# Delta stage of a hybrid attention block: GpSimd's powers placed around the substitution, the diagonal blocks' rates one slot earlier

## The chip, the cores and the metric

The kernel runs on one core of one Trainium2 chip. The metric is the device time of one execution, in microseconds (us), the median of several runs. All data are float32. The engines are TensorE (PE in the profile), VectorE (DVE), ScalarE (ACT), GpSimd (POOL) and SyncE (SP), whose queue issues all the DMA transfers told of here. Each engine runs its own instructions strictly in the order in which they are written; engines meet only at semaphores.

## The reference, cut to what matters

The network is a chain of four residual blocks on (4, 1024, 128) data: a gated delta rule with its own feed-forward, two layers of local attention with feed-forward, a windowed attention, and the two layers once more. The change is in the first of them only, in its recurrent part:

```python
h = _rmsnorm(x, norm1_w)
q = _short_conv_silu(h @ Wq, conv_q_w).reshape(B, T, H, dk)      # H = 8, dk = 96, 4 taps
k = _short_conv_silu(h @ Wk, conv_k_w).reshape(B, T, H, dk)
v = _short_conv_silu(h @ Wv, conv_v_w).reshape(B, T, H, dv)      # dv = 192
q = _l2norm(q) * scale
k = _l2norm(k)
beta = sigmoid(h @ Wb)
g = -exp(A_log) * softplus(h @ Wa + dt_bias)

def step(S, inp):                                                # one token after the other
    q_t, k_t, v_t, g_t, b_t = inp
    S = S * exp(g_t)[..., None, None]
    v_old = einsum('bhk,bhkv->bhv', k_t, S)
    delta = (v_t - v_old) * b_t[..., None]
    S = S + einsum('bhk,bhv->bhkv', k_t, delta)
    return (S, einsum('bhk,bhkv->bhv', q_t, S))

o = _rmsnorm(o, onorm_w) * silu(h @ Wg)
x = x + o @ Wo
```

## The kernel before

**Tiling.** `delta_attention` (the function `delta_prepare` before it makes norms, rates and projections' weights) cuts the 4 x 1024 tokens into 32 chunks of 128 tokens; two chunks make a unit, so there are 16 units. Within a chunk the recurrence is solved as matrices: a triangular 128 x 128 system for each of 8 heads (its inverse ends in `tt`), then a short chain over the state `state`.

**Slots.** Every engine has one loop `for t in range(LAST)`. A unit has 28 slots (`SLOTS`), a chunk 14 (`HALF`); `unit(t, at)` gives the unit whose slot `at` is `t`, and `chunk(t, at)` the chunk, which starts 34 slots (`START`) behind its unit. A number above 27 or an `at` of a chunk therefore falls on some slot of a later unit: an `at` of 12 of a chunk falls on slots 4 and 18 of a unit, 14 on slots 6 and 20, 15 on 7 and 21, 16 and 17 on 8, 9, 22 and 23. In what follows "slot 20" is the slot `t` with remainder 20 by 28. In each slot one tile of k, q or v (8 + 8 + 12 tiles) is projected by TensorE (`L1299`), gets its four convolution taps, and is lit by ScalarE (`L1486`). ScalarE makes the product of the first tap (`L1466`) and of the last (`L1468`), VectorE adds the second and third (`L1623`, `L1631`), and GpSimd adds the last (`L1197`, semaphore `summed`). In slots 16 to 19 (`by_vector`) VectorE adds the last tap too (`L1628`), and GpSimd has no tile.

**What GpSimd does beside the tiles.** In those four slots it solves the 16 x 16 diagonal blocks of the unit's triangular systems (`solve_diagonal`, lines 1182 to 1190, 30 small instructions and a copy, written in four parts of which only the first waits for another engine, for `sub_rates`). Its result goes through memory: SyncE stores it (`L1137`) and loads it back into `t16`, `u16` and `tm`, and TensorE builds the inverse on it from slot 23 on. Further GpSimd raises three things to the power -1/2: the keys' norms `rn` (two halves of 8 columns, slots 15 and 16, `L1206`), and the output's norm `of` of each chunk (8 columns, slots 4 and 18, `L1226`). It makes `bm` for the inverse (slot 21, `L1213`, read by VectorE in slot 23), multiplies the output `o` by the gate in two halves (slots 6, 7, 20, 21; `L1221`, semaphore `o_gated`) and by `of` in two halves (slots 8, 9, 22, 23; `L1233`).

**Who waits for what.** In its slot `t` ScalarE runs `products_of(t)`, then `light(t-1)`, then its other work. Before it writes the gate of the next chunk (slots 8 and 22, `L1494`), it waits for both halves of `L1221`, since they read the gate before. Gate, `vt`, `kq` and the other side results share two banks of PSUM, `misc`, which go round by a table: TensorE claims a bank and waits until the engine that reads it has emptied it. So TensorE waits in slot 23 (`L1353`) for ScalarE's gate of slot 22. `project(t)` also waits for VectorE's taps of tile `t - 2`.

**The diagonal blocks' rates.** After slot 14 SyncE loads the diagonal blocks into `sub` (`L1127`), their diagonals into `n2k` in eight transfers (`L1131`), then `sub_beta` (`L1133`). VectorE turns `n2k` into rates for the whole chunk in slot 15 (`norms`, lines 1674 to 1681), and in slot 16 makes the rates of the diagonal blocks, `sub_rate`, with three small instructions at the end of its slot (`diagonal_rates`, lines 1697 to 1699), for which `solve_diagonal` waits.

Of the kernel before, what the change touches and what calls it, by code (L numbers as in the profile page):

```python
# [821 lines left out]
def delta_attention(nc, name, x_in, dst, w, c):  # L822
# [150 lines left out]
    def unit(t, at):  # L973

        n, rest = divmod(t - at, SLOTS)
        return n if rest == 0 and 0 <= n < UNITS else None
# [103 lines left out]
    def cols(cc):  # L1080
        return slice(cc * H, cc * H + H)

    with nc.Block() as block:

        @block.sync
        def _(sp):
# [15 lines left out]
            for t in range(LAST):  # L1102
# [20 lines left out]
                if n is not None:  # L1123
                    diag_out.need(sp, n)
                    sub_sb.need(sp, n - 1)
                    inv_out.need(sp, n - 1)
                    sp.dma_start(sub[:, 0], diag_d.rearrange("b c h j i -> (b c h) j i")).then_inc(diag_in.sem, 16)  # L1127
                    brk_sb.need(sp, n - 1)
                    for b in range(B16):
                        squares = diag_d[b].rearrange("c h j i -> (j i) (c h)")[0:256:17, :]  # L1130
                        sp.dma_start(n2k[16 * b:16 * b + 16, :], squares, allow_slow_non_contiguous=True).then_inc(n2k_in.sem, 16)  # L1131
                    betas = row_d[1, 2 * H * n:2 * H * (n + 1), :].rearrange("r (b i) -> b r i", i=16)
                    sp.dma_start(sub_beta[:], betas).then_inc(beta_in.sem, 16)  # L1133
# [25 lines left out]
        def _(pool):  # L1159
# [32 lines left out]
            for t in range(LAST):  # L1192
# [10 lines left out]
                for cc in range(2):  # L1203
                    n = unit(t, K_NORM + cc)
                    if n is not None:
                        ins = pool.tensor_tensor(rn[:, n % 2, cols(cc)], n2[:, n % 2, cols(cc)], minus_half[:, 0:H], ALU.pow)  # L1206
                        if cc == 1:
                            ins.then_inc(rn_sb.sem, 1)
                n = unit(t, K_NORM + 6)
                if n is not None:  # L1210
# [3 lines left out]
                                       merge[:].unsqueeze(1).to_broadcast([P, 2 * H, 32]), ALU.mult).then_inc(bm_sb.sem, 1)  # L1214
                for i in range(2):
# [6 lines left out]
                C = chunk(t, 12)  # L1222
                if C is not None:
                    ostat_step.need(pool, C)
                    o_normed.need(pool, C - 1)
                    pool.tensor_tensor(of[:], ostat[:, 1, :], minus_half[:, 0:H], ALU.pow).then_inc(of_sb.sem, 1)  # L1226
# [314 lines left out]
        def _(dve):  # L1541
# [149 lines left out]
            def diagonal_rates(t):  # L1691
                n = unit(t, SOLVE_AT)
# [1240 lines left out]
```

## Time and profile before

| what | us |
|---|---|
| median of 3 runs | 3790.98 |
| lowest and highest of them | 3790.16, 3799.99 |
| the profiled execution | 3798.17 |
| its span (first to last instruction) | 3795.2 |
| in it: before the units' loop | 92.0 |
| the delta stage's loop | 1548.0 |
| the other blocks | 2155.2 |
| TensorE busy over the span | 3294.0 (87%) |
| VectorE | 2723.1 (72%) |
| ScalarE | 2038.1 (54%) |
| GpSimd | 1804.8 (48%) |

Inside the loop (92 to 1640 us) TensorE is busy 1377.0 us, VectorE 1133.4, ScalarE 906.8 and GpSimd 790.2. The times of rows count from the start of the span. A row of the timeline gives the start, the duration, engine, line, operation, what is written and read, shape and count, and in brackets how long the engine sat idle before it and what released it. The shares over the whole kernel say little here: the four engines take turns in being late, slot by slot, so the stretch around one unit's substitution has to be read instruction by instruction.

### The profile page before, as it was taken

To read this page: it belongs to the slowest core of one execution; us is meant where nothing else is said; L and a number is where in the kernel's file an instruction comes from. 1 tells how busy PE (TensorE), PEld (TensorE's weight loads), DVE (VectorE), ACT (ScalarE), POOL (GpSimd) and SP (SyncE) were. 2 spreads that over 40 slices of the span, in tenths; PEclk is the share of its full clock that TensorE was granted. 3 is DMA by queue.
4 is the path that set the end of the run, shared out by engine and by line. 5 is a ranking of instruction groups with operands and counts; after the bars stand their busy time and mean duration, and the time that the engine had idled before them with its cause. 6 is when DMAs were issued, how large, how long until landed. Compare 5 with 4: busy or idle time off the path is not lost. (4 is left out here: it accounts for less than half of the span.)

```text
span 3795.2 us, 87218 instructions
## 1 busy us (share of the span) xinstructions
PE 3294.0 (87%) x32714; PEld 2466.9 (65%) x32714; DVE 2723.1 (72%) x5753; ACT 2038.1 (54%) x4599; POOL 1804.8 (48%) x1647
## 2 busy tenths in 40 slices
PE   4789999999999999968999999986898599899998
PEld 3577777777777777745666566654666366656665
DVE  5577777777777777647777677775999477767775
ACT  3456565656565656513666366632444366636662
POOL 3355555555555555434666166632122466526662
PEclk8689999999999999989999999997999799999999
DMA  4111111111111111033122321222112222131122
GB/s 123 23 24 25 25 25 25 26 25 26 24 27 24 27 25 24 11 95 81 43 53 56 93 50 44 71 79 55 47 50 55 63 49 64 45 95 44 46 71 70
DMA packets 409630, 182.71 MB, mean 48 GB/s; under 512 B 235808, under 2 KB 384384, under 8 KB 406656
## 3 DMA queue, kind: packets, MB, share of 16 engines
q1 hardware_dynamic: 409216, 177.15, 19.0%
q8 instruction: 265, 4.34, 0.5%
q14 instruction: 149, 1.22, 0.1%
HBM read 94.47 MB, written 40.12 MB: 35 GB/s over the span
## 5 line engine op out<-in xcount | busy, mean ns | idle before, releaser
L1197 POOL TENSOR_TENSOR delta_cv<-delta_cv,delta_last_tap 96x256 f32<-96x256 f32 (+1 forms) x384 | 332.7, 867 | 623.4 <-DVE delta_cv L1631 623.4
L1938 POOL TENSOR_TENSOR g_a_rn<-g_a_clip,g_minus_half 128x16 f32<-128x16 f32 x64 | 186.4, 2912 | 271.2 <-DVE g_a_clip L2202 243.0
L1938 POOL TENSOR_TENSOR f_a_rn<-f_a_clip,f_minus_half 128x16 f32<-128x16 f32 x64 | 186.3, 2911 | 260.7 <-DVE f_a_clip L2202 232.5
L2155 ACT ACTIVATE g_a_pr<-g_ps,g_a_nb,g_a_rn 128x128 f32<-128x128 f32 x512 | 185.5, 468 | 146.4 <-DVE g_a_nb L2236 146.4
L2155 ACT ACTIVATE f_a_pr<-f_ps,f_a_nb,f_a_rn 128x128 f32<-128x128 f32 x512 | 185.5, 468 | 146.4 <-DVE f_a_nb L2236 146.4
L1466 ACT ACTIVATE delta_cv<-delta_ps,delta_conv_qk 96x256 f32<-96x256 f32 x256 | 120.9, 472 | 253.5 <-PE delta_ps L1299 252.7
L1623 DVE SCALAR_TENSOR_TENSOR delta_cv<-delta_ps,delta_conv_qk,delta_cv 96x256 f32<-96x256 f32 x256 | 122.1, 477 | 169.5 <-ACT delta_last_tap L1468 169.2
L1243 PE MATMUL delta_ps<-delta_state,delta_qk 96*128 96x192 f32 x1024 | 199.4, 339 | 27.3 <-issue 22.8
L1623 DVE SCALAR_TENSOR_TENSOR delta_cv<-delta_ps,delta_conv_v,delta_cv 128x256 f32<-128x256 f32 x192 | 92.1, 480 | 155.5 <-ACT delta_last_tap L1468 154.1
L1243 PEld LDWEIGHTS delta_ps<-delta_state,delta_qk 96*128 96x128 f32 x1024 | 168.3, 193 | 41.7 <-issue 38.1
L1466 ACT ACTIVATE delta_cv<-delta_ps,delta_conv_v 128x256 f32<-128x256 f32 x192 | 90.5, 471 | 127.5 <-PE delta_ps L1299 127.5
L1486 ACT ACTIVATE delta_vt<-delta_cv 128x256 f32<-128x256 f32 x192 | 80.0, 417 | 136.5 <-DVE delta_cv L1631 84.7
L1941 POOL TENSOR_TENSOR f_a_rot_c<-f_a_rot_c,f_a_rot_s 128x1024 f32<-128x1024 f32 x64 | 150.8, 2357 | 0.0
L1941 POOL TENSOR_TENSOR g_a_rot_c<-g_a_rot_c,g_a_rot_s 128x1024 f32<-128x1024 f32 x64 | 150.8, 2356 | 0.0
L1299 PE MATMUL delta_ps<-delta_ht,delta_wv 128*128 128x259 f32 x384 | 127.7, 423 | 23.6 <-DVE delta_cv L1631 23.6
L2190 DVE TENSOR_TENSOR g_a_rot_c<-g_ps,g_a_table 128x512 f32<-128x512 f32 x128 | 87.8, 686 | 76.5 <-PE g_ps L1972 72.7
L2190 DVE TENSOR_TENSOR f_a_rot_c<-f_ps,f_a_table 128x512 f32<-128x512 f32 x128 | 87.8, 686 | 74.4 <-PE f_ps L1972 70.2
L2230 DVE TENSOR_REDUCE g_a_nmx<-g_ps 128x8 f32<-128x1024 f32 x64 | 78.4, 1225 | 87.5 <-PE g_ps L2028 87.5
L1972 PE MATMUL g_ps<-g_a_wqkv,g_a_ht 128*128 128x512 f32 x256 | 129.9, 631 | 10.8 <-DMA g_a_scales<-L_ffn_k_scale 9.5
L2230 DVE TENSOR_REDUCE f_a_nmx<-f_ps 128x8 f32<-128x1024 f32 x64 | 78.4, 1225 | 84.0 <-PE f_ps L2028 84.0
L1308 PE MATMUL delta_ps<-delta_wg,delta_ht 128*128 128x512 f32 x192 | 100.0, 617 | 38.3 <-ACT delta_vr L1512 38.3
L1631 DVE SCALAR_TENSOR_TENSOR delta_cv<-delta_ps,delta_conv_qk,delta_cv 96x256 f32<-96x256 f32 x256 | 122.9, 480 | 9.1
(350 smaller groups left out, 10477.3 us busy)
## 6 DMA issues: line engine op xcount, KB each, us to landing
f_a_vm<-f_a_v SPq DMA_DIRECT2D x128, 130.0 KB, 2.3
g_a_vm<-g_a_v SPq DMA_DIRECT2D x128, 130.0 KB, 2.3
delta_gd<-delta_dram_row SPq DMA_DIRECT2D x16, 1024.0 KB, 4.6
window_vm<-window_v SPq DMA_DIRECT2D x64, 128.0 KB, 2.3
f_m_x<-y SPq DMA_DIRECT2D x24, 256.0 KB, 3.5
delta_dram_inv<-delta_sub SPq DMA_DIRECT2D x16, 256.0 KB, 2.1
f_m_more<-x SPq DMA_DIRECT2D x16, 256.0 KB, 3.9
x<-f_m_x SPq DMA_DIRECT2D x16, 256.0 KB, 2.3
```

The source lines that it names most:

```text
L1197: pool.tensor_tensor(cv[0:M, t % 3], cv[0:M, t % 3], last_tap[0:M, t % 3], ALU.add).then_inc(summed.sem, 1)
L1243: mm = pe.matmul(ps[0:M, 2 * i + j // 2, j % 2 * DV:(j % 2 + 1) * DV], lhs(h), rhs(h), start=True, stop=True)
L1299: mm = pe.matmul(ps[0:rows_of(k), conv_bank(t), 0:3 + U], lhs, ht[:, n % 3], start=True, stop=True)
L1466: e = act.activation(cv[0:M, t % 3], ps[0:M, conv_bank(t), 0:U], ACT.Copy, scale=taps[:, 0:1])
L1623: dve.scalar_tensor_tensor(out=mine, in0=ps[0:M, conv_bank(t), 1:1 + U], scalar=wts[:, 1:2], in1=mine, op0=ALU.mult, op1=ALU.add).then_inc ...
L1631: dve.scalar_tensor_tensor(out=mine, in0=ps[0:M, conv_bank(t), 2:2 + U], scalar=wts[:, 2:3], in1=mine, op0=ALU.mult, op1=ALU.add).then_inc ...
L1938: pool.tensor_tensor(rn[:, u % 2], clip[:, u % 2], minus_half[:], ALU.pow).then_inc(rn_sb.sem, 1)
L1941: pool.tensor_tensor(rot[:, u % 2], rot_c[:, u % 2], rot_s[:, u % 2], ALU.add).then_inc(rot_sb.sem, 1)
L1972: mm = pe.matmul(ps[:, QK + n, :], tokens, wqkv[:, n * INNER:(n + 1) * INNER], start=True, stop=True)
L2155: e = act.activation(pr[:, u % 2, half, i, :], ps[:, score_bank(u, half), i * P:(i + 1) * P], ACT.Exp, bias=nb[:, u % 2, half, i:i + 1], s ...
L2190: dve.tensor_tensor(rot_c[:, u % 2, r * H:(r + 1) * H, :], ps[:, QK + r, :].rearrange("p (h i) -> p h i", i=DH), cos, ALU.mult)
L2230: dve.tensor_reduce(nmx[:, u % 2].rearrange("p e i -> p (e i)"), ps[:, b0:b0 + 2, :].rearrange("p e (i k) -> p (e i) k", k=P), AX.X, ALU.m ...
```

## The change

Five pieces, all in `delta_attention`; later lines move up by five. `rn` becomes one power over both halves (16 columns) in slot 15. `of` moves from slot 18 and 4 to slot 20 and 6, where it stands ahead of the product with the gate. `bm` moves from slot 21 to slot 22. VectorE makes the diagonal blocks' rates in slot 15, behind `norms`. SyncE loads `sub_beta` ahead of the eight transfers of `n2k`.

```diff
@@ sync
                     sp.dma_start(sub[:, 0], diag_d...).then_inc(diag_in.sem, 16)
+                    betas = row_d[1, 2 * H * n:2 * H * (n + 1), :].rearrange("r (b i) -> b r i", i=16)
+                    sp.dma_start(sub_beta[:], betas).then_inc(beta_in.sem, 16)
                     brk_sb.need(sp, n - 1)
                     for b in range(B16):
                         squares = ...
                         sp.dma_start(n2k[16 * b:16 * b + 16, :], squares, ...).then_inc(n2k_in.sem, 16)
-                    betas = ...
-                    sp.dma_start(sub_beta[:], betas).then_inc(beta_in.sem, 16)
@@ gpsimd
                     n2k_sb.need(pool, n)
                     bvr_sb.need(pool, n - 2)
-                for cc in range(2):
-                    n = unit(t, K_NORM + cc)
-                    if n is not None:
-                        ins = pool.tensor_tensor(rn[:, n % 2, cols(cc)], n2[:, n % 2, cols(cc)], minus_half[:, 0:H], ALU.pow)
-                        if cc == 1:
-                            ins.then_inc(rn_sb.sem, 1)
-                n = unit(t, K_NORM + 6)
+                    pool.tensor_tensor(rn[:, n % 2], n2[:, n % 2], minus_half[:], ALU.pow).then_inc(rn_sb.sem, 1)
+                n = unit(t, K_NORM + 7)
                 if n is not None:
                     rates_sb.need(pool, n)
                     copied(pool, ("x4", n - 1, 1))
                     pool.tensor_tensor(bm[:], ...).then_inc(bm_sb.sem, 1)
+                C = chunk(t, 14)
+                if C is not None:
+                    ostat_step.need(pool, C)
+                    o_normed.need(pool, C - 1)
+                    pool.tensor_tensor(of[:], ostat[:, 1, :], minus_half[:, 0:H], ALU.pow).then_inc(of_sb.sem, 1)
                 for i in range(2):
                     C = chunk(t, 14 + i)
                     ...
-                C = chunk(t, 12)
-                if C is not None:
-                    ostat_step.need(pool, C)
-                    o_normed.need(pool, C - 1)
-                    pool.tensor_tensor(of[:], ...).then_inc(of_sb.sem, 1)
@@ vector
             def diagonal_rates(t):
-                n = unit(t, SOLVE_AT)
+                n = unit(t, SOLVE_AT - 1)
```

GpSimd, unit 1, from the end of the substitution (the copy) to slot 23. `delta_cv` is the addition of a tile's last tap, `delta_o<-delta_o,delta_gate` the product with the gate, `delta_o<-delta_o,delta_of` that with the norm. Before, with the power `delta_of` of this stretch standing 8 rows further up, inside the substitution:

```order
L1190 COPY delta_sub<-delta_sub 128x256
L1197 TENSOR_TENSOR delta_cv<-delta_cv,delta_last_tap 128x256
L1221 TENSOR_TENSOR delta_o<-delta_o,delta_gate 128x768
L1197 TENSOR_TENSOR delta_cv<-delta_cv,delta_last_tap 128x256
L1213 TENSOR_TENSOR delta_bm<-delta_nbrk,delta_merge 128x512
L1221 TENSOR_TENSOR delta_o<-delta_o,delta_gate 128x768
L1197 TENSOR_TENSOR delta_cv<-delta_cv,delta_last_tap 128x256
L1233 TENSOR_TENSOR delta_o<-delta_o,delta_of 128x768
```

and now:

```order
L1190 COPY delta_sub<-delta_sub 128x256
L1197 TENSOR_TENSOR delta_cv<-delta_cv,delta_last_tap 128x256
L1214 TENSOR_TENSOR delta_of<-delta_ostat,delta_minus_half 128x8
L1221 TENSOR_TENSOR delta_o<-delta_o,delta_gate 128x768
L1197 TENSOR_TENSOR delta_cv<-delta_cv,delta_last_tap 128x256
L1221 TENSOR_TENSOR delta_o<-delta_o,delta_gate 128x768
L1197 TENSOR_TENSOR delta_cv<-delta_cv,delta_last_tap 128x256
L1208 TENSOR_TENSOR delta_bm<-delta_nbrk,delta_merge 128x512
L1228 TENSOR_TENSOR delta_o<-delta_o,delta_of 128x768
```

Between the copy and the second product with the gate `delta_bm` has left and the power `delta_of` has come.

VectorE, unit 2, slots 15 and 16. `delta_n`, `delta_brk`, `delta_nbrk` belong to `norms`, `delta_state` is the update of the state, the three rows on `delta_cv` are one tile's taps. Before:

```order
L1677 TENSOR_TENSOR delta_brk<-delta_inv,delta_ex 128x16
L1680 TENSOR_SCALAR delta_nbrk<-delta_brk 128x16
L1681 SCALAR_TENSOR_TENSOR delta_npb<-delta_brk,delta_ex 128x16
L1583 SCALAR_TENSOR_TENSOR delta_state<-delta_state,delta_ex,delta_ps 96x192 x4
L1623 SCALAR_TENSOR_TENSOR delta_cv<-delta_ps,delta_conv_v,delta_cv 128x256
L1628 SCALAR_TENSOR_TENSOR delta_cv<-delta_ps,delta_conv_v,delta_cv 128x256
L1631 SCALAR_TENSOR_TENSOR delta_cv<-delta_ps,delta_conv_v,delta_cv 128x256
L1697 TENSOR_SCALAR delta_sub_rate<-delta_sub 128x16
L1698 RECIPROCAL delta_sub_rate<-delta_sub_rate 128x16
L1699 SCALAR_TENSOR_TENSOR delta_sub_rate<-delta_sub_rate,delta_sub_beta 128x16
```

and now:

```order
L1675 TENSOR_SCALAR delta_nbrk<-delta_brk 128x16
L1676 SCALAR_TENSOR_TENSOR delta_npb<-delta_brk,delta_ex 128x16
L1692 TENSOR_SCALAR delta_sub_rate<-delta_sub 128x16
L1693 RECIPROCAL delta_sub_rate<-delta_sub_rate 128x16
L1694 SCALAR_TENSOR_TENSOR delta_sub_rate<-delta_sub_rate,delta_sub_beta 128x16
L1578 SCALAR_TENSOR_TENSOR delta_state<-delta_state,delta_ex,delta_ps 96x192 x4
L1618 SCALAR_TENSOR_TENSOR delta_cv<-delta_ps,delta_conv_v,delta_cv 128x256
L1623 SCALAR_TENSOR_TENSOR delta_cv<-delta_ps,delta_conv_v,delta_cv 128x256
L1626 SCALAR_TENSOR_TENSOR delta_cv<-delta_ps,delta_conv_v,delta_cv 128x256
```

The three instructions of the rates have moved ahead of one half of the state's update (four instructions) and of one tile's taps.

## Rows read from the trace of the kernel before

**Rows 1.** Stretches of two neighbouring units: length, busy us, granted clock (PEclk), DMA share, GB/s.

```profile
842.30:933.90 91.60, 82.74 (x774) 70.72 (x773) 70.74 (x150) 57.01 (x144) 49.87 (x68) 0.98 0.12 26
933.90:1030.00 96.10, 87.04 (x774) 74.43 (x773) 72.08 (x156) 57.00 (x144) 49.90 (x68) 0.93 0.12 25
```

**Rows 2.** Timeline of GpSimd, unit 7, slots 15 and 16.

```profile
769.57 1.65 POOL L1206 TENSOR_TENSOR delta_rn<-delta_n,delta_minus_half 128x8 f32<-128x8 f32 x1
773.31 0.73 POOL L1182 TENSOR_TENSOR delta_sub<-delta_sub,delta_sub_rate 128x256 f32<-128x256 f32 x1 [2.10 <-DVE delta_sub_rate L1699]
...
776.00 1.65 POOL L1206 TENSOR_TENSOR delta_rn<-delta_n,delta_minus_half 128x8 f32<-128x8 f32 x1
```

**Rows 3.** Timeline of GpSimd, unit 7, slot 18 to slot 21.

```profile
783.51 1.65 POOL L1226 TENSOR_TENSOR delta_of<-delta_ostat,delta_minus_half 128x8 f32<-128x8 f32 x1
...
787.23 0.61 POOL L1190 COPY delta_sub<-delta_sub 128x256 f32<-128x256 f32 x1
787.80 0.73 POOL L1197 TENSOR_TENSOR delta_cv<-delta_cv,delta_last_tap 128x256 f32<-128x256 f32 x1
788.48 1.81 POOL L1221 TENSOR_TENSOR delta_o<-delta_o,delta_gate 128x768 f32<-128x768 f32 x1
790.25 0.72 POOL L1197 TENSOR_TENSOR delta_cv<-delta_cv,delta_last_tap 128x256 f32<-128x256 f32 x1
790.93 1.05 POOL L1213 TENSOR_TENSOR delta_bm<-delta_nbrk,delta_merge 128x512 f32<-128x512 f32 x1
791.93 1.81 POOL L1221 TENSOR_TENSOR delta_o<-delta_o,delta_gate 128x768 f32<-128x768 f32 x1
```

**Rows 4.** Timeline of ScalarE there, slots 21 and 22.

```profile
788.56 0.42 ACT L1486 ACTIVATE delta_vt<-delta_cv 128x256 f32<-128x256 f32 x1 [2.36 <-POOL delta_cv L1197]
...
793.78 1.08 ACT L1494 ACTIVATE delta_gate<-delta_ps 128x512 f32<-128x512 f32 x2 [2.35 <-POOL delta_o L1221]
```

**Rows 5.** The waits, 280 to 1580 us: total us, times, longest.

```profile
ACT delta_gate L1494 <- POOL delta_o L1221: 43.6, 28, 2.4
```

**Rows 6.** Timeline of TensorE there, slot 23.

```profile
794.52 0.52 PE L1353 MATMUL delta_ps<-delta_ident,delta_vt 128*128 128x128 f32 x3 [0.66 <-ACT delta_gate L1494]
```

**Rows 7.** Timeline of VectorE, unit 7, slots 15 and 16.

```profile
768.73 0.16 DVE L1674 TENSOR_SCALAR delta_n<-delta_n2k 128x16 f32<-128x16 f32 x1
...
769.67 0.17 DVE L1680 TENSOR_SCALAR delta_nbrk<-delta_brk 128x16 f32<-128x16 f32 x1
...
772.57 0.16 DVE L1697 TENSOR_SCALAR delta_sub_rate<-delta_sub 128x16 f32<-128x16 f32 x1
```

**Rows 8.** The same, the last adding instruction of tiles 20 and 21.

```profile
784.66 0.48 DVE L1631 SCALAR_TENSOR_TENSOR delta_cv<-delta_ps,delta_conv_v,delta_cv 128x256 f32<-128x256 f32 x1
...
787.33 0.48 DVE L1631 SCALAR_TENSOR_TENSOR delta_cv<-delta_ps,delta_conv_v,delta_cv 128x256 f32<-128x256 f32 x1
```

**Rows 9.** The DMA issues of SyncE, unit 7, slot 15.

```profile
761.62 3.87 SPq L1131 DMA_DIRECT2D delta_n2k<-delta_dram_diag  x8
765.53 0.60 SPq L1133 DMA_DIRECT2D delta_sub_beta<-delta_dram_row  x1
```

**Rows 10.** The page, costliest groups: a power over 16 columns in another stage.

```profile
L1938 POOL TENSOR_TENSOR f_a_rn<-f_a_clip,f_minus_half 128x16 f32<-128x16 f32 x64 | 186.3, 2911 | 260.7 <-DVE f_a_clip L2202 232.5
```

**Rows 11.** Stretches of 4 us with the granted clock, units 7 and 8.

```profile
790.00:794.00 4.00, 3.86 (x12) 2.71 (x10) 0.97 (x2) 0.97 (x3) 4.00 (x5) 0.62 0.27 26
...
822.00:826.00 4.00, 4.00 (x46) 3.22 (x43) 3.96 (x9) 3.39 (x10) 2.25 (x2) 0.50 0.00 0
```

**Rows 12.** Timeline of all engines, unit 9, slots 7 to 9.

```profile
933.97 0.72 POOL L1197 TENSOR_TENSOR delta_cv<-delta_cv,delta_last_tap 96x256 f32<-96x256 f32 x1 [1.40 <-DVE delta_cv L1631]
...
936.51 1.09 ACT L1494 ACTIVATE delta_gate<-delta_ps 128x512 f32<-128x512 f32 x2 [0.77 <-POOL delta_o L1221]
...
940.68 1.74 DVE L1600 TENSOR_SCALAR delta_q_eps<-delta_q_sum 128x8 f32<-128x8 f32 x1
...
940.93 1.46 POOL L1233 TENSOR_TENSOR delta_o<-delta_o,delta_of 128x768 f32<-128x768 f32 x1
```

More of the change, by code:

```diff
@@ L1131, in _ @@
                         sp.dma_start(n2k[16 * b:16 * b + 16, :], squares, allow_slow_non_contiguous=True).then_inc(n2k_in.sem, 16)
-                    betas = row_d[1, 2 * H * n:2 * H * (n + 1), :].rearrange("r (b i) -> b r i", i=16)
-                    sp.dma_start(sub_beta[:], betas).then_inc(beta_in.sem, 16)
                 n = unit(t, SOLVE_AT + 4)
@@ L1221, in _ @@
                         pool.tensor_tensor(mine, mine, gate[:, HB * i * DV:HB * (i + 1) * DV], ALU.mult).then_inc(o_gated.sem, 1)
-                C = chunk(t, 12)
-                if C is not None:
-                    ostat_step.need(pool, C)
-                    o_normed.need(pool, C - 1)
-                    pool.tensor_tensor(of[:], ostat[:, 1, :], minus_half[:, 0:H], ALU.pow).then_inc(of_sb.sem, 1)
                 for i in range(2):
```

## The prediction

> **What bounds the kernel now.** The page's shares name no single engine, so I read the delta stage's loop in units. Two neighbouring units take 91.6 and 96.1 us with the same work [rows 1]; that difference is taken up under the clock. Then I read one unit (unit 7) engine by engine from slot 15 to slot 23, looking for the engine that never waits. It is GpSimd. It starts the substitution at 773.31 after 2.10 us of idleness, in which it waits for VectorE's rates [rows 2], and from there it has no idle time until its second product with the gate ends at 791.93 + 1.81 = 793.74 [rows 3]. Two others wait for it: ScalarE stands 2.36 us for tile 20's last tap and 2.35 us for that second product before it may write the gate, at 793.78 [rows 4], and TensorE's next work of slot 23 starts at 794.52, released by ScalarE's gate [rows 6]. The wait of the gate occurs 28 times in 1300 us, twice a unit, 43.6 us in all [rows 5]: 2.35 us here, and 0.77 us in slot 8 [rows 12]. So around the substitution the time of a slot is set by the length of GpSimd's list, and the last wait is that of ScalarE's gate in slot 22.
>
> **Part 1, the substitution itself.** It runs from 773.31 to 787.23 + 0.61 = 787.84, 14.53 us [rows 2, 3]. Two powers of 1.65 us lie in it, the second half of `rn` at 776.00 and `of` at 783.51. Without them 14.53 - 3.30 = 11.23 us remain. The new start: one power over 16 columns takes the place of 8 columns at 769.57. The kernel has that shape elsewhere with 2.91 us [rows 10]; the bounds are 1.65 us (a column count that costs nothing) and 3.30 us (twice the 8 columns). I take 2.91, the row of the same shape: 769.57 + 2.91 = 772.48. The rates are no longer waited for: `norms` is past its fourth instruction at 769.67 and two more follow [rows 7], so the rates, 0.74 us long by the distance from 772.57 to GpSimd's start at 773.31, are there at about 770.7. End of the substitution: 772.48 + 11.23 = 783.71, 4.1 us earlier; by the bounds 782.4 to 784.1.
>
> **Part 2, what is late next.** Not all of the 4.1 us count. GpSimd's next instruction adds tile 20's last tap, for which VectorE must end at 784.66 + 0.48 = 785.14 [rows 8]. VectorE works without a break over slots 16 to 19, and the rates only change places in its list, so I leave that time. GpSimd now idles about 1.4 us there; this also covers either bound of the 16-column power. Then come, back to back: tap 20 (0.73), `of` (1.65), first product (1.81), tap 21 (0.72; its input ends at 787.81, long before), second product (1.81) [rows 3, 8]. That is 6.72 us, ending at 785.14 + 6.72 = 791.86. Before, it was 793.74. `bm` (1.05 us) has left this list for slot 22. **Gain: 1.88 us a unit.** Had `of` been left out of this list too, it would be 3.5; the change gives 1.65 us of it back. The stretch after slot 22 is a shifted copy: ScalarE's gate starts 1.88 us earlier, TensorE's slot 23 as well. `bm` would end near 791.86 + 0.73 + 1.05 = 793.6, and VectorE reads it in slot 23, after TensorE's work that follows 794.52 - 1.88 = 792.64 and ScalarE's tile in between, so I cost its move at nothing; the cover is about 1 us. Units 1 to 15 have chunk work in slots 20 and 21 (unit 0 has none and is counted at zero): 15 x 1.88 = **28.2 us**.
>
> **Part 3, the small moves.** VectorE's rates in slot 15 push one half of the state's update and tile 16's taps back by 0.74 us, and nothing after them, since the rates stood there anyway. Who waits: TensorE's transposes of slot 17. Bound 0 to 0.74 us a unit; I take 0, because VectorE runs without idle time through slot 19 and is what the others wait for there. SyncE issues `sub_beta` 0.60 us long ahead of eight transfers that now end at 765.49 and then at 766.09 [rows 9]; VectorE reads them at 768.73 [rows 7] without a wait. Cost 0, at most 0.6. In slots 4 to 9 the power `of` leaves slot 4 and stands ahead of the product in slot 6: GpSimd's 1.40 us of idleness ahead of tile 7 [rows 12] take up most of 1.65 us, 0.25 us are left to reach the gate of slot 8, which already waits 0.77 us for GpSimd. Bounds 0 and 1.65 us a unit; I take 0, since 0.25 us is less than the slack of the tiles around it (TensorE's projection is the next wait of ScalarE). Both ends stay in the range.
>
> Does a small VectorE instruction stand still beside a GpSimd power? The trace has both answers. `L1680` starts at 769.67, inside the power that began at 769.57, and takes 0.17 us [rows 7, 2]; `L1600` starts at 940.68 and takes 1.74 us, until GpSimd's 768-column product of 940.93 is over at 942.39 [rows 12]. The rates have the form of `L1680`, and their neighbour is a power, so I take 0.17. The Trainium skill (SBUF — State Buffer, Who interferes with whom) says that VectorE's `tensor_scalar` in a two-port mode shares a port pair with GpSimd, which is held for the whole instruction. By that rule the time would be that of rival D; the row of `L1600` agrees with it for long products, the row of `L1680` does not for powers.
>
> **Part 4, the clock.** Granted clock drops twice in a unit's neighbourhood. One low stretch falls on slots 21 to 22 (mean 0.62 of full in 790 to 794, 2.4 GHz being full and 1.2 GHz the low level), after TensorE stood still; it costs nothing now, since TensorE waits for the gate anyway. A second one (0.50 in 822 to 826) [rows 11] comes after the tiny matrices of the inverse in slots 2 and 3, and only in every other unit: it is the difference between 96.1 and 91.6 us, 4.5 us [rows 1]; seven of the units 1 to 14 have it. The work is the same in both, so where it falls depends on how the units lie in time, and a unit 1.9 us shorter moves it. Bounds: in no unit (-7 x 4.5 = -31.5 us) and in all 15 (+8 x 4.5 = +36 us). I take 4 of 15, -13.5 us: the present order looks like a lock that brings it back each second unit, and without that lock it should be rarer. Against this, TensorE's idle time in slots 22 to 23 is now over sooner and the first low stretch can reach work on the path; 4 us at 0.62 lose 4 x 0.38 = 1.5 us [rows 11]. Bounds 0 to 1.5 us a unit, I take a third, 0.55: +8.3 us. The clock together: -5 us.
>
> **The sum.** 28.2 + 5.2 = 33.4 us off. The profiled execution took 3798.17 us, 7.2 over the median of the runs; this gives 3764.8 for it and 3790.98 - 33.4 = **3757.6 us** for the median.
>
> **Rivals.** (A) The second low stretch goes altogether and the first stays harmless: 28.2 + 31.5 = 59.7 us off, 3731. For it speaks that one half of the units are free of it already at the same work; against it that the low activity in slots 2 and 3 stays. Chance 0.17. (B) GpSimd's gain is given back at another place. In slot 23 GpSimd would run product, tap and product back to back (1.46 + 0.73 + 1.46 us), and `L1600`, which falls there, could stand for two of them; or `of` in slot 6 reaches the gate of slot 8 with more than 0.25 us. With 1.4 us a unit returned, 15 x 0.48 = 7 us stay: 3784. Against it speaks that VectorE has idle time behind `L1600`. Chance 0.18. (C) Slower: the low clock falls on slots 2 to 5 in every unit and on TensorE's path in slot 23 as well, +36 + 15 x 1.5 = +58.5 us against 28.2: 3821. It decides in this direction from 28 us of clock loss on; for it, that the pattern of today is kept by the units' length, which changes; against it, that both must come together. Chance 0.06. (D) The rates stand still beside the power as `L1600` does beside a product. Then they begin at 772.48 instead of 769.9, VectorE's whole list of slots 16 to 20 is 2.5 us late, tile 20's taps with it, and 1.88 - 2.5 = -0.6 us a unit are left: 15 x 0.6 = 9 us more, less 5 for the clock, 3795. The row of `L1680` speaks against it, the unbroken list of VectorE for its price. Chance 0.08.
>
> **How the numbers follow.** The forecast, 3745 to 3772, has 0.51. The range takes it in, rival A down to its price and rival B up to a little over its price: 3731 to 3786. A measurement of this kernel can tell 0.3%, 11.4 us, from no change. Faster by more than that (under 3779.6): the forecast, A and half of B, 0.77. Within it: half of B and D, 0.17. Slower: C, 0.06.
>
> **What would show it.** Right: GpSimd's substitution starts without a wait for the rates and is over about 4 us sooner against the taps of tile 20; a new idle time of 1 to 1.5 us ahead of tile 20's last tap; ScalarE's wait for tile 20 gone, its wait for the gate in slot 22 still there and about 1.9 us earlier; units without the second low stretch near 89.7 us. Wrong: a 16-column power well over 3.3 us, `L1692` (the rates' first instruction) far longer than 0.17 us, a wait of `bm`'s reader in slot 23, or units that differ in length in another pattern than by 4.5 us.

## The result, and the profile after

The kernel after takes 3778.45 us (median of 8 runs, 3757.21 to 3786.40), the kernel before beside it 3796.11 us (8 runs, 3786.49 to 3802.89). The ratio is 0.9948 with an interval of 0.9927 to 0.9969: faster by 0.5%, 17.7 us by the medians. The forecast was 33.4 us off, 3757.6 us. The direction is right and the time lies in the range of 3731 to 3786, but not in its middle part, 3745 to 3772; about half of the gain is missing. The profiled execution of after took 3786.40 us with a span of 3784.6 us. It is the slowest of the eight, 8 us above their median.

**The units.** The same view as in [rows 1], stretches with their busy times and granted clock, for units of after. A unit runs here from the end of one substitution's copy to the end of the next.

```profile
961.10:1054.90 93.80, 85.08 (x779) 72.93 (x778) 71.64 (x155) 57.48 (x146) 49.52 (x68) 0.96 0.12 26
1147.70:1237.50 89.80, 81.08 (x775) 69.39 (x774) 71.92 (x155) 57.08 (x146) 49.52 (x68) 1.00 0.13 26
1237.50:1333.30 95.80, 88.42 (x773) 76.23 (x772) 71.07 (x149) 56.97 (x145) 49.48 (x67) 0.91 0.12 25
```

The unit from 1147.70 has full clock throughout and takes 89.8 us, where 89.7 was forecast and 91.6 stood in [rows 1]. But of the units 1 to 14 only three are within 1 us of that; the others take 91.5 to 97.6 us, where before there were 91.6 and 96.1 and one of 97.8. The steps of the change are read in the undisturbed unit first.

**The power and the rates, slot 15.** Timeline of GpSimd, after; then of VectorE at the same place.

```profile
1132.85 0.72 POOL L1197 TENSOR_TENSOR delta_cv<-delta_cv,delta_last_tap 96x256 f32<-96x256 f32 x1 [2.34 <-DVE delta_cv L1626]
1133.53 2.91 POOL L1203 TENSOR_TENSOR delta_rn<-delta_n,delta_minus_half 128x16 f32<-128x16 f32 x1
1136.41 0.72 POOL L1182 TENSOR_TENSOR delta_sub<-delta_sub,delta_sub_rate 128x256 f32<-128x256 f32 x1
```

```profile
1133.17 0.43 DVE L1672 TENSOR_TENSOR delta_brk<-delta_inv,delta_ex 128x16 f32<-128x16 f32 x1
1133.63 0.17 DVE L1675 TENSOR_SCALAR delta_nbrk<-delta_brk 128x16 f32<-128x16 f32 x1
...
1133.81 0.17 DVE L1692 TENSOR_SCALAR delta_sub_rate<-delta_sub 128x16 f32<-128x16 f32 x1
...
1134.29 0.17 DVE L1694 SCALAR_TENSOR_TENSOR delta_sub_rate<-delta_sub_rate,delta_sub_beta 128x16 f32<-128x16 f32 x1
```

The 16-column power takes the 2.91 us of [rows 10]; the substitution (`L1182`) starts right behind it, with no bracket for an idle time, where it had waited 2.10 us [rows 2]. The three rates run inside the power at 0.17 and 0.25 us.

**Slots 20 to 22.** GpSimd, after, from the substitution's copy on: to be held against [rows 3].

```profile
1147.10 0.61 POOL L1190 COPY delta_sub<-delta_sub 128x256 f32<-128x256 f32 x1
1149.20 0.73 POOL L1197 TENSOR_TENSOR delta_cv<-delta_cv,delta_last_tap 128x256 f32<-128x256 f32 x1 [1.49 <-DVE delta_cv L1626]
1149.88 1.66 POOL L1214 TENSOR_TENSOR delta_of<-delta_ostat,delta_minus_half 128x8 f32<-128x8 f32 x1
1151.50 1.83 POOL L1221 TENSOR_TENSOR delta_o<-delta_o,delta_gate 128x768 f32<-128x768 f32 x1
1153.27 0.75 POOL L1197 TENSOR_TENSOR delta_cv<-delta_cv,delta_last_tap 128x256 f32<-128x256 f32 x1
1153.96 1.83 POOL L1221 TENSOR_TENSOR delta_o<-delta_o,delta_gate 128x768 f32<-128x768 f32 x1
1155.72 0.74 POOL L1197 TENSOR_TENSOR delta_cv<-delta_cv,delta_last_tap 128x256 f32<-128x256 f32 x1
1156.40 1.07 POOL L1208 TENSOR_TENSOR delta_bm<-delta_nbrk,delta_merge 128x512 f32<-128x512 f32 x1
```

GpSimd, which never waited here, now stands 1.49 us for VectorE ahead of tile 20. From there to the end of the second product, 1149.20 to 1155.79, the list is 6.59 us long. ScalarE beside it, to be held against [rows 4]:

```profile
1150.06 0.41 ACT L1481 ACTIVATE delta_vt<-delta_cv 128x256 f32<-128x256 f32 x1
...
1154.05 0.42 ACT L1481 ACTIVATE delta_vt<-delta_cv 128x256 f32<-128x256 f32 x1 [2.22 <-POOL delta_cv L1197]
1155.82 1.09 ACT L1489 ACTIVATE delta_gate<-delta_ps 128x512 f32<-128x512 f32 x2 [1.35 <-POOL delta_o L1221]
```

The wait for tile 20 is gone (the first row), a wait of 2.22 us for tile 21 has come, because `of` and a product stand ahead of its last tap, and the gate's own wait is 1.35 instead of 2.35 us. Rows of the waits over 280 to 1580 us, the first of before, the other two of after. The last answers to [rows 5]; the wait of TensorE for the gate has grown from 7.1 to 34.6 us:

```profile
PE delta_ps L1353 <- ACT delta_gate L1494: 7.1, 14, 0.7
...
PE delta_ps L1348 <- ACT delta_gate L1489: 34.6, 14, 2.6
ACT delta_gate L1489 <- POOL delta_o L1221: 31.1, 27, 1.4
```

**TensorE around slot 23.** This is where the missing half is. First before, unit 7, TensorE ahead of and behind the row of [rows 6]:

```profile
789.65 1.12 PE L1308 MATMUL delta_ps<-delta_wg,delta_ht 128*128 128x512 f32 x2 [2.70 <-ACT delta_vr L1512]
790.61 2.39 PE L1243 MATMUL delta_ps<-delta_vr,delta_tt 128*128 128x192 f32 x8
792.79 1.07 PE L1299 MATMUL delta_ps<-delta_ht,delta_wv 128*128 128x259 f32 x2
...
795.01 1.12 PE L1365 MATMUL delta_ps<-delta_t,delta_al 64*64 64x32 f32 x32
796.06 1.57 PE L1243 MATMUL delta_ps<-delta_vr,delta_tt 128*128 128x192 f32 x8
```

Then after, the undisturbed unit:

```profile
1151.15 1.13 PE L1303 MATMUL delta_ps<-delta_wg,delta_ht 128*128 128x512 f32 x2 [0.23 <-ACT delta_vr L1507]
...
1156.56 0.52 PE L1348 MATMUL delta_ps<-delta_ident,delta_vt 128*128 128x128 f32 x3 [2.55 <-ACT delta_gate L1489]
1157.05 1.12 PE L1360 MATMUL delta_ps<-delta_t,delta_al 64*64 64x32 f32 x32
1158.10 1.57 PE L1238 MATMUL delta_ps<-delta_vr,delta_tt 128*128 128x192 f32 x8
1159.51 0.60 PE L1294 MATMUL delta_ps<-delta_ht,delta_wv 128*128 128x259 f32 x2
```

And the same rows of after in the unit of 93.8 us, with its stretches of 4 us and their granted clock:

```profile
970.82 0.52 PE L1348 MATMUL delta_ps<-delta_ident,delta_vt 128*128 128x128 f32 x3 [2.55 <-ACT delta_gate L1489]
971.31 1.85 PE L1360 MATMUL delta_ps<-delta_t,delta_al 64*64 64x32 f32 x32
973.09 2.93 PE L1238 MATMUL delta_ps<-delta_vr,delta_tt 128*128 128x192 f32 x8
```

```profile
968.00:972.00 4.00, 1.45 (x20) 1.03 (x20) 0.78 (x3) 2.34 (x6) 4.00 (x5) 0.93 0.36 37
972.00:976.00 4.00, 4.00 (x31) 3.94 (x29) 1.49 (x4) 1.52 (x4) 3.26 (x3) 0.50 0.13 33
```

Before, TensorE stood 2.70 us ahead of slot 21's work and only 0.66 us ahead of slot 23 [rows 6]. The low clock of [rows 11] followed the long wait and fell on products (2.39 us where 1.57 is the full-clock time) that were over before the gate came. After, the first wait has shrunk to 0.23 us, and the long one, 2.55 us, stands directly ahead of slot 23. TensorE is busy 1.45 of the 4 us from 968, and then the clock is 0.50, which is the 1.2 GHz level, on work that all other engines wait for: the inverse's 32 small matmuls take 1.85 instead of 1.12 us, the eight products 2.93 instead of 1.57.

**A third stretch.** The record of the granted clock has one more low stretch, 80 to 93 us behind the end of the substitution, around the next substitution (slots 16 to 19). Before, none of the units 1 to 14 has it; after, nine have. It makes TensorE's projections late, ScalarE's products of the last tap with them, and so VectorE's taps of tile 20. VectorE in after ahead of tile 20, first in front of the unit from 961.1, with this stretch, then in front of the undisturbed one:

```profile
962.39 0.48 DVE L1618 SCALAR_TENSOR_TENSOR delta_cv<-delta_ps,delta_conv_v,delta_cv 128x256 f32<-128x256 f32 x1 [1.38 <-ACT delta_last_tap L1463]
...
1148.11 0.48 DVE L1618 SCALAR_TENSOR_TENSOR delta_cv<-delta_ps,delta_conv_v,delta_cv 128x256 f32<-128x256 f32 x1 [0.90 <-ACT delta_last_tap L1463]
```

GpSimd's wait for tile 20 is then 1.9 to 3.2 us instead of 1.5, in seven of the 14 units, 5.8 us in all; it is 2.34 us in the unit of 93.8 us.

### The profile page after: what moved, and what is told of

Read it like the earlier page. It is cut to its first block and busy times, and to the rows that moved or that the text cites. A ratio compares the mean times of both kernels' runs of the same rounds, so it can differ in the third digit from the quotient of the medians.

```text
span 3784.6 us, 87201 instructions
## 1 busy us (share of the span) xinstructions
PE 3303.1 (87%) x32714; PEld 2481.1 (66%) x32714; DVE 2725.0 (72%) x5753; ACT 2038.9 (54%) x4599; POOL 1798.9 (48%) x1631
## 5 line engine op out<-in xcount | busy, mean ns | idle before, releaser
L1967 PE MATMUL f_ps<-f_a_wqkv,f_a_ht 128*128 128x512 f32 x256 | 129.0, 627 | 0.0
```

The source lines that it names most:

```text
L1967: mm = pe.matmul(ps[:, QK + n, :], tokens, wqkv[:, n * INNER:(n + 1) * INNER], start=True, stop=True)
```

## Experiments

In each table row below the ratio is against the kernel before, measured beside it; times of different rows are compared by these ratios.

| label | what it is | median us | ratio (interval) |
|---|---|---|---|
| after_again | the kernel after | 3771.93 | 0.9960 (0.9942 to 0.9978) |
| f_before | before + fillers | 3795.53 | 1.0001 (0.9989 to 1.0013) |
| f_after | after + fillers | 3764.83 | 0.9921 (0.9908 to 0.9935) |
| f_ofback | f_after, `of` at its old place | 3744.28 | 0.9864 (0.9851 to 0.9877) |
| f_bmback | f_after, `bm` in slot 21 again | 3774.08 | 0.9947 (0.9934 to 0.9961) |
| f_rates | rates and load of `sub_beta` moved alone, + fillers | 3757.98 | 0.9898 (0.9885 to 0.9912) |
| f_powers | powers, `bm` and that load moved, rates not, + fillers | 3762.42 | 0.9910 (0.9896 to 0.9923) |
| p_rates | rates and load moved alone | 3762.09 | 0.9929 (0.9916 to 0.9941) |
| ofback | after, `of` at its old place | 3725.57 | 0.9815 (0.9800 to 0.9829) |
| g_ofback | ofback + one filler | 3725.99 | 0.9808 (0.9790 to 0.9826) |
| g_after | after + one filler | 3769.86 | 0.9953 (0.9939 to 0.9967) |
| g2_after | after + two fillers | 3755.20 | 0.9889 (0.9872 to 0.9905) |

### Fillers in both kernels: f_before, f_after

Two theories on the missing half: the clock took it, or GpSimd's gain is returned at another place (rival B). To tell them apart both kernels get fillers: products that nobody reads, written to columns of PSUM that are written anew before anyone reads them. They stand where TensorE stood still or did little, ahead of tile 23 and ahead of the products of slots 2 and 5. For `y5`, one of these products, the claim of the bank is also moved ahead of two waits.

```diff
@@ tensor, ahead of the projection of tile t; k is the tile's number
+                if k == 23:
+                    for r in range(2):
+                        pe.matmul(ps[:, conv_bank(t), :], ident[:], wg[:, r * 512:(r + 1) * 512], start=True, stop=True)
@@ tensor, product y, behind its claim of a bank; the same in y5
+                    pe.matmul(ps[:, bank, 256:512], ident[:], wg[:, 0:256], start=True, stop=True)
```

> The kernel before, with extra TensorE products whose results nobody reads, put where TensorE waits in any case: two of 512 columns ahead of tile 23, one of 256 columns ahead of the last product y, one of 256 ahead of each y5. They are to hold the granted clock at its full level through the loop. Theory (GpSimd's list, and beside it the clock): without the low stretches of slots 2 to 5 every unit takes what the clean units took, 91.6 us, plus some tenths for the fillers; 7 x 4.5 us less and more at the start, about 3765 (1.008 times faster). Rival (the length of units isn't the clock's doing): fillers only add, 3796 to 3810.

> The changed kernel with the same fillers. Theory (GpSimd's list is 1.88 us shorter in each of 15 units, and in the plain kernels the clock takes half of it back): 28 us under the filled kernel before, units of 89.7 to 90 us throughout, about 3735. Rival 1 (the gain is only another pattern of the clock): the same time as the filled kernel before, within 5 us. Rival 2 (the list gives only what the plain kernels differ by, 1.2 us a unit): 18 us less.

f_before takes 3795.53 us: no gain over before, where about 3765 was looked for. The fillers do remove the stretch of slots 2 to 5 from all of units 1 to 14, but they cost 1.3 us in every unit (92.9 against 91.6 us, all of it in slots 2 to 5), and in five units the low stretch of slots 21 and 22 is still there and runs into the fillers, which makes them 94.1 us. Together this eats the gain. As a remedy it is a miss. As an instrument it works in the main: the stretch of slots 2 to 5 and that on slot 23 are gone from the units 1 to 14 of both kernels, though the clock is not the same everywhere, since f_after has the third stretch in seven units. Units of f_before, f_after, f_ofback, f_bmback, f_rates and f_powers:

```profile
596.88:689.77 92.89, 84.88 (x784) 71.40 (x784) 71.94 (x157) 57.21 (x144) 49.86 (x70) 1.00 0.12 26
```

```profile
766.87:857.87 91.00, 86.00 (x786) 72.97 (x785) 71.95 (x155) 57.13 (x146) 49.41 (x68) 0.98 0.13 26
```

```profile
853.86:943.81 89.95, 84.56 (x786) 71.45 (x785) 70.71 (x150) 57.22 (x144) 49.55 (x69) 1.00 0.12 27
```

```profile
682.76:774.74 91.98, 84.81 (x786) 71.37 (x785) 71.86 (x155) 56.99 (x146) 49.46 (x68) 1.00 0.12 26
```

```profile
491.87:582.67 90.80, 84.81 (x785) 71.40 (x785) 70.70 (x150) 57.23 (x145) 49.81 (x70) 1.00 0.12 26
```

```profile
584.68:675.78 91.10, 84.88 (x786) 71.41 (x785) 72.05 (x156) 57.11 (x145) 49.45 (x68) 1.00 0.12 26
```

f_after against f_before: 1.9 us a unit, between these two as between the means of all 14 (93.3 and 91.4), and 30.7 us by the medians. The 1.88 us of the prediction's Part 2 and its 28.2 us are there in full when the low clock is kept off slots 2 to 5 and 23. Nothing of them is returned elsewhere: rival B falls, and the missing half is the clock's.

### One piece undone: f_ofback, f_bmback

```diff
@@ gpsimd, f_ofback: the power stands behind the product with the gate, in slot 18
-                C = chunk(t, 14)
+                C = chunk(t, 12)
@@ gpsimd, f_bmback
-                n = unit(t, K_NORM + 7)
+                n = unit(t, K_NORM + 6)
```

> The filled changed kernel with the power `of` back in slots 4 and 18 (behind its old neighbours), all else as changed. Theory: in slot 18 it is covered by GpSimd's 1.4 us of idleness ahead of tile 20, in slot 20 it isn't. The substitution ends 1.65 us later, tile 20 starts 0.2 later, and the second product with the gate ends 1.4 us earlier than in the changed kernel: up to 1.4 x 15 = 21 us under the filled changed kernel, less if VectorE's taps of tile 22 or ScalarE are then late (they allow at least 1 us). Rival (moving `of` out of the substitution is what makes the gain): slower by 1.65 x 15 = 25 us.

> The filled changed kernel with `bm` back in slot 21, ahead of the second product with the gate. Theory: 1.05 us more in the list for which ScalarE waits, 15 x 1.05 = 16 us over the filled changed kernel. Rival (the wait of ScalarE's gate is no longer on the path after the change): no difference within 4 us.

With `of` back in slot 18, inside the substitution, a unit is 1.0 us shorter than in f_after, and the time is 20.5 us less (3744.28 against 3764.83 us). The substitution is 12.9 instead of 11.3 us long, but that only fills the 1.5 us in which GpSimd waited for tile 20, and `of` is gone from the list behind it. In the profiled executions the units carry 12.9 us of this; another 7.8 us come behind the last substitution, which was not followed up. So moving `of` harms. The merging of `rn` was not undone by itself. With `bm` back in slot 21, ahead of the second product, the gate waits for it again. ScalarE, f_bmback:

```profile
783.88 1.09 ACT L1494 ACTIVATE delta_gate<-delta_ps 128x512 f32<-128x512 f32 x2 [2.35 <-POOL delta_o L1221]
```

That is 1.0 us a unit, the length of `bm`, as costed. By the medians it is only 9.3 us, not some 16; the profiled spans differ by 14.7 us (3779.4 and 3764.7), so the units carry it, and the medians' difference is smaller than they explain.

### Each half of the change alone: f_rates, f_powers

```diff
@@ f_rates: before + beta's load first, and in the vector part
-                n = unit(t, SOLVE_AT)
+                n = unit(t, SOLVE_AT - 1)
@@ f_powers: after, but the rates in slot 16 as before
-                n = unit(t, SOLVE_AT - 1)
+                n = unit(t, SOLVE_AT)
```

> The filled kernel before (fillers as in the other filled kernels) with one part of the change: the diagonal blocks' rates in slot 15 and the load of sub_beta first. Powers and bm as before. Theory (GpSimd's list): the substitution starts at the end of the first half of rn, 2.1 us earlier, and everything behind it in the list moves with it, since tile 20's taps are not reached: 2.1 us a unit under the filled kernel before, units of 90.8 us against 92.9 and 91.0 of the filled change, about 3795 - 31 = 3764: this part alone gives all that the change gives. Rival (the parts add up, each its own share): 0.83 us a unit, the share by which the start of the substitution moved in the changed kernel, units of 92.1 us, about 3782.

> The filled changed kernel with the rates back in slot 16: only the powers and bm moved (and sub_beta loaded first). Theory: the substitution starts at 773.3 as before on the scale of unit 7 and ends at 784.6, still ahead of the taps of tile 20 at 785.1; the list behind is the same: 91.0 us a unit, the time of the filled changed kernel within 3 us. Rival (the parts add up): 0.8 us a unit slower than the filled changed kernel, 12 us more.

Either half gives what both give: units of 90.8 and 91.1 us, against 91.0 for the whole (f_after) and 92.9 for f_before. Two rows say why the halves don't add. GpSimd at tile 20 in f_rates, then in f_powers:

```profile
582.63 0.73 POOL L1197 TENSOR_TENSOR delta_cv<-delta_cv,delta_last_tap 128x256 f32<-128x256 f32 x1
```

```profile
676.54 0.72 POOL L1197 TENSOR_TENSOR delta_cv<-delta_cv,delta_last_tap 128x256 f32<-128x256 f32 x1 [0.75 <-DVE delta_cv L1631]
```

f_rates takes away only the 2.10 us wait of [rows 2], keeps the substitution at 14.5 us, and reaches tile 20 without idle time. f_powers still waits 0.8 to 1.2 us for the rates and nevertheless stands 0.75 us ahead of tile 20; the whole change stands 1.5 us there. VectorE's last adding instruction of tile 20 is the floor of f_powers and of the whole change. f_rates comes 0.5 us behind it (it is over at 582.13) and has no `of` behind it in its list.

### Without fillers: ofback, p_rates, after_again

> The changed kernel once more, to stand beside the next two on the same chip: 3770 to 3785, clean units of 89.75 us, most units 2 to 6 us longer, with a low clock in slots 23 and 24.

> No fillers: the changed kernel with the power `of` back in slots 4 and 18. Theory: its clean units are 1.0 us shorter than those of the changed kernel (88.7), as in the filled pair (90.0 against 91.0), so 15 to 20 us under 3778 if the clock takes the same part, about 3760; where the low stretches fall can move that by 20 us either way. Rival (the clock eats every gain of this kind): 3778.

> Without fillers: the kernel before with the rates in slot 15 and sub_beta loaded first, nothing else. Theory: clean units of 91.6 - 2.1 = 89.5 us, so never worse in GpSimd's list than the full change (89.75); with the clock as it falls, 3750 to 3785. Rival (only the full change brings a gain on this kernel): within 5 us of the kernel before.

ofback, which is the kernel after with `of` back at its old place and nothing else, is with g_ofback the fastest of all: 3725.57 us, 0.9815 (0.9800 to 0.9829) of before, and the version to keep. A unit of it, and TensorE in slot 23:

```profile
1112.47:1200.79 88.32, 81.02 (x775) 69.33 (x773) 71.41 (x156) 57.04 (x144) 49.52 (x69) 1.00 0.13 27
```

```profile
1118.33 0.52 PE L1348 MATMUL delta_ps<-delta_ident,delta_vt 128*128 128x128 f32 x3 [1.13 <-ACT delta_gate L1489]
```

Its undisturbed unit is 1.4 us shorter than that of after, and TensorE's wait ahead of slot 23 is 1.4 us shorter too, 1.13 us. Fifteen units at 1.4 us are 21 us. By the ratios ofback is 1.3 to 1.5% ahead of after, 50 to 55 us. The rest, some 30 us, is in the main clock that ofback doesn't lose: by the table further down, 16.7 us are lost in it, where after loses 53.5 and 37.6. p_rates, measured beside after_again, is ahead of it too, 3762.09 to 3771.93 us (0.9929, 0.9916 to 0.9941, and 0.9960, 0.9942 to 0.9978), although its undisturbed unit (89.5 us) is much the same as that of after; its wait in slot 23 is 2.0 us.

### The wait itself: g_after, g2_after, g_ofback

If TensorE's wait of 2.55 us ahead of slot 23 brings the low clock onto that slot, then filling it with work that nobody reads, and changing nothing else, must give the time back. g_after and g_ofback have one filler of 512 columns ahead of tile 23, g2_after two.

```diff
@@ tensor, ahead of the projection of tile t: g_after, g_ofback; g2_after has the line for wg[:, 512:1024] too
+                if k == 23:
+                    pe.matmul(ps[:, conv_bank(t), :], ident[:], wg[:, 0:512], start=True, stop=True)
```

> The changed kernel with `of` back and one filler only, a product of 512 columns ahead of tile 23, where TensorE waits. Theory (the clock is lost at two places, after slot 22 and after slots 2 and 3, and the fillers in slots 2, 3 and 5 cost 1.3 us a unit): the low stretch after slot 22 goes at no cost, that after slots 2 and 3 stays in some units; 3740 to 3755. Rival (only the fillers of slots 2, 3 and 5 hold the clock): 3760 as without fillers.

> The changed kernel with one filler: a product of 512 columns ahead of tile 23, in the 2.5 us in which TensorE waits for the gate. Theory (the gain that is missing was lost because TensorE's wait in slots 22 and 23 is followed by a low clock, now on the path): the low stretch at +10 us from the end of the substitution goes in most units, those units shorten by 2 to 4 us, and 20 to 35 us come off the changed kernel, about 3750. Rival (the missing gain was lost somewhere else, in slots 6 to 9 or at the moved bm): the filler changes nothing beyond 5 us, since it only fills a wait.

> The changed kernel with both 512-column products ahead of tile 23 and none of the other fillers. With one of them the low stretch at +10 us stayed in 8 of 14 units; with both and the others it was in none. Theory (the low clock at +10 us is the answer to TensorE's wait in slots 22 and 23): it is gone from at least 12 of 14 units, and clean units stay at 89.8 to 90.3 us; the stretch at +37 us comes in some units with 4.5 us each, so 3745 to 3762. Rival (the fillers of slots 2, 3 and 5 held the clock, not those ahead of tile 23): the stretch at +10 us stays in half of the units, 3765 to 3775.

One filler missed: g_after takes 3769.86 us, no different from after_again (3771.93), where 3750 was expected. Two fillers hit: 3755.20 us, 0.9889 (0.9872 to 0.9905) of before, against 0.9960 for after_again. TensorE in g2_after, slot 22 to slot 23:

```profile
857.31 1.88 PE L1292 MATMUL delta_ps<-delta_wg,delta_ident 128*128 128x512 f32 x4
859.02 0.60 PE L1297 MATMUL delta_ps<-delta_ht,delta_wv 128*128 128x259 f32 x2
860.44 0.52 PE L1351 MATMUL delta_ps<-delta_ident,delta_vt 128*128 128x128 f32 x3 [0.81 <-ACT delta_gate L1492]
860.93 1.12 PE L1363 MATMUL delta_ps<-delta_t,delta_al 64*64 64x32 f32 x32
861.98 1.57 PE L1238 MATMUL delta_ps<-delta_vr,delta_tt 128*128 128x192 f32 x8
```

The gate comes as late as before the fillers; only the time until then is filled, and slot 23 runs at full clock. In g_ofback the filler changes nothing (3725.99), since there the wait was short already; it is 0.3 us with it.

Over all kernels without fillers in slots 2 and 5 the wait and the low clock on slot 23 go together. The wait alone does not decide it, though: f_bmback, with all fillers, still waits 1.8 us ahead of slot 23 and has the low clock there in none of 14 units, where g_after with 1.7 us has it in 8. The last three columns count units 1 to 14 of the profiled executions by the record of the granted clock: low about 8 to 12 us behind the substitution's end (slots 22 to 24), low about 33 to 39 us behind it (slots 2 to 5), and the time lost, which is the length of the 14 units less 14 undisturbed ones and has the third stretch in it. The wait is the usual one; some units of before and of ofback have half of it. The undisturbed unit of before, 91.6 us, has the low stretch of slots 21 and 22, which costs it nothing.

| kernel | wait ahead of slot 23, us | low at slot 23 | low at slots 2 to 5 | lost, us |
|---|---|---|---|---|
| after | 2.55 | 11 | 5 | 53.5 |
| after_again | 2.55 | 11 | 2 | 37.6 |
| p_rates | 2.0 | 8 | 2 | 26.9 |
| g_after | 1.7 | 8 | 3 | 31.9 |
| ofback | 1.1 | 1 | 2 | 16.7 |
| g2_after | 0.8 | 0 | 2 | 14.1 |
| g_ofback | 0.3 | 0 | 3 | 18.7 |
| before | 0.7 | 1 | 7 | 33.4 |

(1310.7 - 14 x 89.8 = 53.5 for after; 1315.8 - 14 x 91.6 = 33.4 for before.) In g_after and p_rates the low stretches on slot 23 are all of the shorter kind, over in about 3 us; in after five of the eleven are twice as long.

## Why the prediction was half right

**Part 1, right.** The power over 16 columns took 2.91 us as taken from [rows 10], and the substitution 11.3 us (11.23 forecast). It starts without a wait.

**Part 2, right, and to the tenth.** Idle time ahead of tile 20: 1.49 us (about 1.4 forecast). The list behind it: 6.59 us (6.72). The undisturbed unit: 89.8 us (89.7). With fillers in both kernels, 1.9 us a unit and 30.7 us in all (1.88 and 28.2). The remark that leaving `of` out of the list would give 3.5 us a unit was right as well: it gives 3.3 us (91.6 to 88.3, ofback) and 2.9 us under fillers (92.9 to 89.95, f_ofback). What the prediction did not see is that with `of` moved the halves of the change overlap, so that either alone carries nearly all of it.

**Part 3, right.** In slot 8 ScalarE waits 0.94 us for the product with the gate, 0.17 more than in [rows 12]; 0.25 was the estimate and 1.65 the upper bound.

```profile
1202.68 1.08 ACT L1489 ACTIVATE delta_gate<-delta_ps 128x512 f32<-128x512 f32 x2 [0.94 <-POOL delta_o L1221]
```

`bm` is over at 1157.47, and VectorE reads it at 1158.58 (`L1703`), so its cover was 1.1 us (about 1). The rates cost 0.17 us beside the power; over all 16 units `L1692` takes 165 to 170 ns and `L1694` 174 to 176, and rival D is excluded. The Trainium skill (SBUF — State Buffer, Who interferes with whom) says that a VectorE instruction with two inputs in SBUF contends with a GpSimd instruction that reads SBUF. The row of `L1672`, 0.43 us and over when the tap's addition of 1132.85 is, agrees; the row of `L1694`, 0.17 us in the middle of the power, does not. The measurement decides: this power does not hold VectorE up.

**Part 4, wrong in size and in sign.** The term was -5.2 us: +8.3 for the first low stretch (0.55 us a unit, bounds 0 to 1.5) and -13.5 for the second (4 of 15 units in place of 7). Measured: the lost time of units 1 to 14 went from 33.4 to 53.5 us in the profiled execution, +20.1 us, and to 37.6 us in that of after_again, +4.2. The mis-sized term is the first stretch. Taking out the second at 4.4 us a unit (92.7 against 88.3 us in g_ofback) and the longer waits for tile 20 (5.8 and 6.3 us), about 26 and 22 us are left for the first, as much as its upper bound of 15 x 1.5 = 22.5 us or more. That bound was worked out from 4 us at a clock of 0.62, that is, from the length that the stretch showed on work with slack. On slot 23 it costs 1.7 us where it is short (91.5 against 89.8 us) and 3.1 where it is long (92.8 us, the unit from 1054.9), and it is there in 11 of 14 units. The prediction had "TensorE's idle time in slots 22 to 23 is now over sooner" and did not ask where that idle time goes. It had read the 0.66 us of [rows 6], and of the wait two slots ahead it had only that TensorE stood still, not its 2.70 us. The change doesn't shorten TensorE's idle time there by much, 3.36 to 2.78 us; it gathers it in one place, right ahead of the slot that everybody waits for. The second stretch was sized well within its bounds: 5 and 2 units in the two executions, against 4. The third was not foreseen. The prediction's own sign of being wrong, units that differ in another pattern than by 4.5 us, did come.

**The sum as it came.** In the profiled executions: undisturbed units 14 x (89.8 - 91.6) = -25.2, clock +20.1, and the first unit -9.9 (98.0 to 88.1 us), which had been counted at zero. The granted clock over that unit rose from 0.69 to 0.74, so the clock has a part in it; with the fillers in both kernels the first unit gained 3.8 us. It was not split further. Together -15.0 us, of which the times show 11.8 (3798.17 to 3786.40). 1.3 us more are gained ahead of it and 5.6 us lost again behind the last substitution; that was not followed up. That the time came into the range is in part luck: the first unit, on which the forecast did not count, is 9.9 of these 11.8 us, and in after_again 10.3 of the 28.7 us by which the span is shorter.

**What stays open.** Shown is that filling the wait ahead of slot 23, and nothing else, takes the low clock off that slot (g2_after, in one profiled execution). Not shown is how long a wait has to be, which f_bmback speaks against as the only measure, and what decides in which of otherwise equal units it falls: the units at 961.1 and at 1147.7 have the same wait of 2.55 us, and one is low behind it and the other isn't. This also makes the kernel restless: its runs reach from 3757 to 3786 us in one set of 8 and from 3759 to 3793 in another of 11, and those of g2_after, only four, from 3750 to 3756.

## What to carry to other kernels

When a change makes one engine's list shorter, look at where TensorE's idle time goes and not only at how long it is: gathered in one piece ahead of the work that all wait for, it brought a low clock there that cost some 22 to 26 us, where the shorter list had brought 25; in the units behind the first a gain was left only because another low stretch became rarer. Ask of each moved piece whether it leaves the list that ends last or only changes its place in it; here the rates alone carried as much as the whole change, and the move of `of` took 1.4 us a unit back. To tell a list's gain from the clock's share, compare units that the low clock leaves alone, or put unread products into TensorE's waits in both kernels and compare those.

## What the runs showed of the hardware

- A wait of TensorE of 2.55 us with little work around it was followed by the 1.2 GHz level in 11 of 14 units (after and after_again), one of 2.0 us (p_rates) or 1.7 us (g_after) in 8, one of 1.1 us in one (ofback) and one of 0.8 us in none (g2_after). It is not the wait alone: with fillers in slots 2 and 5 too, 1.8 us were followed by it in none (f_bmback), and the wait of 2.7 us ahead of slot 21 was followed by it in 13 of 13 units of before and in 5 of 13 of f_before.
- The price depends on what lies behind the wait: nothing in before, 1.7 to 3.1 us a unit in after.
- Unread matmuls can pay: two of 512 columns in a wait gave 14 units free of low clock in slot 23 and about 0.7% of the time (ratios 0.9889 and 0.9960). With the 256-column ones in slots 2 and 5 as well, a unit of before was 1.3 us longer, and nothing was gained (ratio 1.0001).
- GpSimd's power takes longer with more columns, 1.65 us for 8 and 2.91 us for 16, and small VectorE instructions run inside it at their usual 0.17 us.
